# Gate weights of the first and third expert mixture fetched from device memory instead of formed by a matmul

## The reference, cut to what matters

```python
# layer 0 (32 experts of width 64, top 8, one shared expert), gate weights topk_w [rows, 8]
g = einsum('th,eih->eti', x, expert_gate); u = einsum('th,eih->eti', x, expert_up)
outs = einsum('eti,ehi->eth', silu(g) * u, expert_down)
final = (gathered * topk_w[:, :, None]).sum(1) + shared(x)
# layer 2 (32 experts, top 4, capacity 128 rows an expert), gate weights w
h = silu(xe @ W1) * (xe @ W3); ye = h @ W2
out = (ye[eid, posc] * gflat[:, None]).reshape(-1, K, D).sum(1) + shared(X)
```

## Time and profile before

| | |
|---|---|
| median of 3 runs | 866.2 us (862.1 to 868.02) |
| profiled execution | 867.06 us, span 865.3 us |
| PE / PEld busy | 759.5 us (88%) / 539.0 us (62%) |
| DVE busy | 553.4 us (64%) |
| ACT / POOL busy | 375.8 us (43%) / 390.4 us (45%) |
| mean granted PE clock | 0.939 of full speed |
| first W matmul / last W matmul | 120.2 us / 719.6 us after the start |

### The profile page before, as it was taken

How to read it: one execution, slowest core, us unless ns; L and a number is a source line. 1 busy time by engine, 2 the same in 40 slices (tenths; PEclk the granted TensorE clock), 3 DMA queues, 4 the chain that set the end, 5 groups by cost and what they waited for, 6 DMA issues and landing times.

```text
span 865.3 us, 13644 instructions
## 1 busy us (share of the span) xinstructions
PE 759.5 (88%) x3936; PEld 539.0 (62%) x3936; DVE 553.4 (64%) x1813; ACT 375.8 (43%) x834; POOL 390.4 (45%) x381
## 2 busy tenths in 40 slices
PE   6989889999999878976979787999989989798995
PEld 3467767676767546654969786565645544555663
DVE  3377877777788378862633575978776655344554
ACT  0234344444445435625545334547455565313441
POOL 2000024544546434363674343655445665253772
PEclk8799989999999969966999998999999999899999
DMA  5021899930000121014677651000330000013325
GB/s 146 1 62 50 267 333 332 333 88 0 1 1 1 53 57 30 21 47 146 172 208 211 195 167 50 10 1 1 83 101 14 13 10 17 10 41 78 101 70 146
DMA packets 74394, 79.34 MB, mean 92 GB/s; under 512 B 17769, under 2 KB 61424, under 8 KB 74194
## 3 DMA queue, kind: packets, MB, share of 16 engines
q1 hardware_dynamic: 68112, 69.49, 27.8%
q0 software_dynamic: 5024, 8.54, 2.9%
q10 hardware_dynamic: 1186, 0.43, 0.2%
HBM read 40.48 MB, written 39.85 MB: 93 GB/s over the span
## 4 chain that ended last, share of the span: by engine, by line
PE 60%; DVE 22%; issue 7%; POOL 4%; ACT 3%; DMA 3%; SPq 1%; ACTq 0%; DVEq 0%; POOLq 0%
PE psum L1186 54%; PE psum L1635 1%; POOL s L754 1%; DVE hb L2328 1%; DVE hb L2329 1%; DVE hb L2326 1%; DVE mr L1984 1%; DVE const L1940 1%; POOL s L732 1%; PE psum L1245 1%; DMA chosen<-in_mask_1x1xSxS_ik 1%; DVE wk L1941 1%; PE psum L1373 1%; DVE l_lo L1900 1%; DMA l_hi<-y 1%
## 5 line engine op out<-in xcount | busy, mean ns | idle before, releaser
L1186 PE MATMUL psum<-xt_hi,wa_hi 128*128 128x512 f32 x272 | 129.0, 474 | 9.7 <-DVE hb L2329 5.0
L691 POOL TENSOR_TENSOR h_lo<-hb,h_hi 128x512 fp32r<-128x512 f32 x68 | 87.7, 1293 | 83.1 <-ACT h_hi L920 82.8
L759 POOL DMA_INDIRECT y<-xn x93 | 92.2, 992 | 64.7 <-DVE xn L2076 33.6
L902 ACT ACTIVATE hb<-psum 128x512 f32<-128x512 f32 x136 | 81.0, 596 | 86.3 <-PE psum L1186 85.7
L1186 PE MATMUL psum<-xt_lo,wa_hi 128*128 128x512 f32 x272 | 108.4, 399 | 0.0
L686 POOL TENSOR_TENSOR hb<-hb,wsb 128x512 f32<-128x512 f32 x64 | 82.3, 1286 | 56.6 <-DVE hb L2326 51.5
L662 POOL TENSOR_TENSOR rstd<-veps,neghalf 128x4 f32<-128x4 f32 x20 | 20.3, 1017 | 130.0 <-DVE veps L1878 129.6
L1186 PEld LDWEIGHTS psum<-xt_hi,wa_hi 128*128 128x128 f32 x272 | 52.7, 194 | 31.6 <-DVE hb L2329 9.5
L2326 DVE TENSOR_TENSOR hb<-hb,psum 128x512 f32<-128x512 f32 x68 | 46.0, 684 | 40.0 <-ACT hb L902 29.5
L1186 PE MATMUL psum<-hb,wa_hi 128*128 128x512 f32 x136 | 70.9, 602 | 0.5 <-POOLq L688 0.5
L1186 PEld LDWEIGHTS psum<-xt_lo,wa_hi 128*128 128x128 f32 x272 | 52.5, 193 | 16.2 <-issue 7.5
(11 more groups left out here) (353 smaller groups left out, 1706.9 us busy)
## 6 DMA issues: line engine op xcount, KB each, us to landing
s<-l_lo SPq DMA_DIRECT2D x20, 1386.0 KB, 16.5
l_hi<-in_pack SPq DMA_DIRECT2D x24, 322.0 KB, 3.4
l_lo<-in_pack SPq DMA_DIRECT2D x22, 322.0 KB, 3.4
xn<-s SPq DMA_DIRECT2D x93, 66.0 KB, 2.0
stage<-in_pack SPq DMA_DIRECT2D x13, 256.0 KB, 2.7
y_in<-y SPq DMA_DIRECT2D x8, 256.0 KB, 3.8
l_hi<-y SPq DMA_DIRECT2D x8, 256.0 KB, 4.9
stage<-in_L_ffn_W SPq DMA_DIRECT2D x12, 128.0 KB, 2.4
```

The source lines that it names most:

```text
L691: pool.tensor_tensor(h_lo[:, k % 3, :], hb[:, k % 4, :], h_hi[:, k % 3, :].bitcast(F32), ALU.subtract).then_inc(q["hlo_pool"], 1)
L759: pool.indirect_dma_start(y3, bass.IndirectOffsetOnAxis(xe3[:, j % XE, 128:129].bitcast(I32), 0), xe3[:, j % XE, 0:128], None, bounds_chec ...
L902: act.activation(hb[:, k % 4, :], G[k % 2][:, :], ACT.Silu).then_inc(q["sg_done"], 1)
L1186: return pe.matmul(o, l, r, start=start, stop=stop, skip_group_check=True)
```

## The change

- `comb_in` turns the f32 weights `wfin` (32 rows) in place of the three bf16 parts; `route_end` is one instruction in layer 0 and ends one product after the capacity test in layer 2.
- `pre_comb` copies them to `wt0`; a DMA writes `wt0` to a new tensor `wd` in device memory (SP issues it for layer 0, ACT for layer 2), and SP then reads, for each routed unit, two rows of `wd`, each repeated over 64 partitions, into SBUF: eight buffers `wrow` in layer 0, the three buffers `wsb` in layer 2.
- The W matmul, its PSUM banks, `comb_t` and ACT's copy of W go away. In layer 0 the freed banks make G and U three deep, and DVE multiplies by `wrow` (SBUF). In layer 2 POOL multiplies by `wsb` as before, but waits for the DMA.
- The shared expert becomes the first chunk of a sequence.
- The 20 pattern fills are spread: 3 first, then 4 in each of three sequences, then 5. The loads of layer 3's weights go from SP to ACT, at unit 40 of layer 2.
- Routing steps of layer 2 and the Fourier steps that lie in it are put in other units; in the `chain` everything from `pt` on comes one step later.

```diff
-            back1=42, rows5=42, upd1=43, xt5=44, low5=45, logits5=46, score5=47, choose5=48, cum5=49, end5=50)
+            back1=42, rows5=42, upd1=43, xt5=44, low5=44, logits5=45, score5=46, choose5=47, cum5=48, end5=48, comb5=49)
-CH = dict(mom6=0, scl6=3, xt6=4, scores=5, exp=6, norm=7, pt=7, ptc=8, val=8, up=9, scl7=12, xt7=13, logits=14, top=15,
+CH = dict(mom6=0, scl6=3, xt6=4, scores=5, exp=6, norm=7, pt=8, ptc=9, val=9, up=10, scl7=13, xt7=14, logits=15, top=16,
...
+        G0, U0 = [bank[i] for i in (0, 1, 4)], [bank[i] for i in (2, 3, 5)]
...
+            return (c - 1, 15 + c, 31 + c) if c else (48, 49, 50)
...
-        ROUTE_AT = {0: (5, 6, 7, 9, 10, 11, 11, 12, 12), 2: (8, 8, 8, 8, 8, 9, 10, 11, 12)}
-        WEIGH_AT = {0: 13, 2: 14}
-        COMBT_AT = {0: 15, 2: 16}
-        PE_XN, PE_LOGITS, PE_RUN, PE_COMB = {0: 0, 2: 2}, {0: 1, 2: 5}, 11, {0: 12, 2: 13}
+        ROUTE_AT = {0: (5, 6, 7, 9, 10, 11, 11, 12, 12), 2: (8, 8, 8, 8, 8, 9, 9, 9, 10)}
+        WEIGH_AT = {0: 13, 2: 11}
+        COMBT_AT = {0: 15, 2: 13}
+        PE_XN, PE_LOGITS, PE_RUN, PE_COMB = {0: 0, 2: 2}, {0: 1, 2: 5}, 8, {0: 13, 2: 10}
...
-                return 2 + b, (4, 7, 8, 11, 10, 13)
+                return 2 + b, (6, 9, 12, 14, 14, 16)
...
+            def gate_rows(b, c):
+                w = b * ROUTED[0] + c
+                if w >= WS:
+                    pb, pc = divmod(w - WS, ROUTED[0])
+                    sp.wait_ge(q["h_done"], hnum(0, pb, pc + 1) + 1)
+                for e in range(2):
+                    sp.dma_start(wrow[64 * e:64 * e + 64, w % WS, :],
+                                 wd[b, 2 * c + e:2 * c + e + 1, :].broadcast_to([64, S])).then_inc(d_wb[w % WS], 16)
+
+            def gate_weights():
+                ...
+                for b in range(B):
+                    sp.wait_ge(q["combt_done"], fnum(0, b))
+                    sp.dma_start(wd[b], wt0[:, :]).then_inc(d_wt, 16)
+                    sp.wait_ge(d_wt, WT0 + 16 * (b + 1))
+                    for c in range(ROUTED[0]):
+                        gate_rows(b, c)
+                        if b + 1 < B and c in Z_AFTER:
+                            zero_rows(Z_FIRST + b * len(Z_AFTER) + Z_AFTER.index(c))
...
+            for b in range(B):
+                sp.wait_ge(d_wt2, WT2 + 16 * (b + 1))
+                for c in range(ROUTED[2]):
+                    w = b * ROUTED[2] + c
+                    if w >= 3:
+                        sp.wait_ge(q["w_used"], w - 2)
+                    for e in range(2):
+                        sp.dma_start(wsb[64 * e:64 * e + 64, w % 3, :],
+                                     wd[b, 2 * c + e:2 * c + e + 1, :].broadcast_to([64, S])).then_inc(d_w1[w % 3], 16)
...
-                    pool.wait_ge(q["wcopy_done"], w + 1)
+                    pool.wait_ge(d_w1[w % 3], WB2[w % 3] + 32 * (w // 3 + 1))
...
+                act.activation(wt0[:, :], T[0:32, :], ACT.Copy).then_inc(q["combt_done"], 1)
+                if l == 2:
+                    act.wait_ge(q["combt_done"], fnum(l, b))
+                    act.dma_start(wd[b], wt2[:, :]).then_inc(d_wt2, 16)
...
+            def load_layer3():
+                act.wait_ge(q["x_done"], x_num(4, 3))
+                for i, w in enumerate(("routed_w1", "routed_w2", "routed_w3")):
+                    act.dma_start(pk3[:, :, F3 * i:F3 * i + F3], a["L3_ffn_" + w].rearrange("e d h -> d e h")).then_inc(d_wl, 16)
...
+                if l == 0:
+                    if k >= 3:
+                        pe.wait_ge(q["sg_done"], k - 2)
+                    product(G0[k % 3][:, :], gs).then_inc(q["g_done"], 1)
+                    if k >= 3:
+                        pe.wait_ge(q["um_done"], k - 2)
+                    product(U0[k % 3][:, :], us).then_inc(q["u_done"], 1)
+                    return
...
-                    last = mm(W[0 if l == 2 else k % 2][:, :], pick, comb_t[0:3 * N_EXP[l], b % 2, :], True, True)
...
+                if l == 0:
+                    dve.tensor_tensor(wfin[:, :, :], w_, wrec[:, :].unsqueeze(2).broadcast_to([128, TB, E]),
+                                      ALU.mult).then_inc(q["comb_done"], 1)
+                    return
...
-                for j in range(2):
-                    link(dve.tensor_copy(chl[:, :, E * j:E * j + E], w_))
-                    ...
+                    dve.tensor_tensor(wfin[:, :, :], w_, m_, ALU.mult).then_inc(q["comb_done"], 1)
...
-                    link(dve.tensor_tensor(h, h, U[k % 2][:, :], ALU.mult))
-                    dve.tensor_tensor(h, h, W[k % 2][:, :], ALU.mult).then_inc(q["h_done"], 1)
+                dve.tensor_tensor(h, h, U0[k % 3][:, :], ALU.mult).then_inc(q["um_done"], 1)
+                ...
+                dve.wait_ge(d_wb[w % WS], 32 * (w // WS + 1))
+                dve.tensor_tensor(h, h, wrow[:, w % WS, :], ALU.mult).then_inc(q["h_done"], 1)
```

More of the change, by code:

```diff
@@ L53 @@
 ROWS_AHEAD = 3
+Z_FIRST = 3
+Z_AFTER = (8, 10, 12, 14)
 ZR = 3
@@ L95 @@
 SH_DOWN = {SH_AT + t: n for n, t in enumerate((11, 17, 22))}
-COUNT_PE = [SH_AT + t for t in (17, 18, 19)]
+COUNT_PE = [SH_AT + t for t in (18, 19, 20)]
 C_ID, C_HEAD, C_TRI, C_SEL, C_SEL16, C_SEL8, C_DFT = 0, 128, 144, 272, 304, 320, 328
@@ L210, in link, with build @@
         self.eng.wait_ge(self.sem, self.n)
-def build(nc, a, out, s1, s3, y3, stages=8):
+def build(nc, a, out, s1, s3, y3, wd, stages=8):
     with ExitStack() as ctx:
@@ L308, in build @@
         d_x = [sem(f"d_x{b}") for b in range(B)]
+        d_wt, WT0 = d_wnat, 16 * 4
+        d_wb, W1_BASE = d_w1, 32 * (B * ROUTED[0] // WS)
+        d_wt2, WT2 = d_wnat, 16 * (4 + B)
+        WB2 = [W1_BASE + 16 * len(range(i, NB1, WS)) for i in range(3)]
         d_stage = [sem(f"d_stage{i}") for i in range(2)]
@@ new lines, in gate_rows @@
+            def gate_rows(b, c):
[7 more added lines that the diff above has]
+            def gate_weights():
+                sp.wait_ge(q["zp_set"], 2)
+                for i in range(Z_FIRST):
+                    zero_rows(i)
+                for b in range(B):
[6 more added lines that the diff above has]
+                            zero_rows(Z_FIRST + b * len(Z_AFTER) + Z_AFTER.index(c))
@@ L565, in _ @@
             for r in range(NQ):
                 if r == NQ0:
-                    sp.wait_ge(q["zp_set"], 2)
-                    for rows, s in ((ROWS1 // 128, s1), (ROWS3 // 128, s3)):
-                        flat = s.rearrange("(p r) c -> p (r c)", p=128)
-                        for z in range(0, rows, ZCHUNK):
-                            n = min(ZCHUNK, rows - z)
-                            dst = flat[:, ROW3 * z:ROW3 * (z + n)].rearrange("p (r c) -> p r c", c=ZR * ROW3)
-                            sp.dma_start(dst, zpat.unsqueeze(1).broadcast_to([128, n // ZR, ZR * ROW3])).then_inc(d_zero, 16)
+                    gate_weights()
@@ L574, in _ @@
                 if r == NQ0 + 2:
+                    for i in range(Z_FIRST + (B - 1) * len(Z_AFTER), NZ):
+                        zero_rows(i)
                     sp.wait_ge(q["x_done"], x_num(1, 3))
@@ L1107, in _ @@
                         context_out(i)
+                        if stages > 1 and i == 15:
+                            pre_comb(0, 0)
                         if i < 12:
@@ L1153, in _ @@
                             k = b * NC[l] + c
[L1154 to L1156 removed]
+                            if l == 2 and k == L3_AT:
+                                load_layer3()
+                            if l != 2 and k >= 1:
                                 pb, pc = divmod(k - 1, NC[l])
@@ L1418, in comb_in @@
             def comb_in(l, b):
-                rows = 3 * N_EXP[l]
                 pe.wait_ge(q["comb_done"], fnum(l, b))
@@ L1422, in comb_in @@
                 for k in range(TB):
-                    last = pe.transpose(T[:, :].bitcast(BF16)[0:rows, 128 * k:128 * k + 128], chl[:, k, 0:rows], ident_bf[:, :])
+                    last = pe.transpose(T[0:32, 128 * k:128 * k + 128], wfin[:, k, :], ident)
                 last.then_inc(q["combt_ps"], 1)
@@ L1762, in _ @@
                             values0(i - 1)
+                        if stages > 1 and i == 15:
+                            comb_in(0, 0)
                         if i < 12:
@@ L2640 @@
     y3 = nc.dram_tensor("y3", (2 * B * S, D), F32, kind="Internal").ap()
-    build(nc, a, out, s1, s3, y3, STAGES)
+    wd = nc.dram_tensor("wd", (B, 32, S), F32, kind="Internal").ap()
+    build(nc, a, out, s1, s3, y3, wd, STAGES)
     r = run_bass_kernel_spmd(nc, [arrays], core_ids=[0])
```

112 lines of the change are left out of this document (41 added, 71 removed).

## The result

The changed kernel is slower: 884.34 us median (879.78 to 894.81, four runs) against 864.15 for the kernel before on the same chip; the ratio is 1.020, 95% interval 1.0158 to 1.0242. The forecast was 852 us.

A forecast was written before the change was run, and what follows sets the result against it. PE was taken to bound most of both mixtures, DVE next. Terms -8, -1.2, -8.7, -1.5, -2, +1.5 and +6 sum to -13.9; 867.1 less 13.9 and 0.9 (profiled execution above median) gives 852 us, range 828 to 870.

The forecast's parts named there:

- Layer 0, -8: Layer 0: W matmuls and split go, DVE's gate product and POOL take turns; sequences of 43.2 us, -8 us in all.
- The bound for PE alone: Layer 0: a sequence takes 39.0 us if PE alone decides, without the W matmuls.
- The fetch in layer 0, 0: Layer 0: gate rows' round trip of 6.2 us is covered by 1 us; 0, range 0 to +9 us.
- Entry of layer 2, -1.2 and "0, at worst +3": Layer 2's start: split leaves PE's path, -1.2 us; first gate row's round trip hides behind other units, 0, at worst +3.
- POOL's wait for gate rows, +1.5: Layer 2: POOL waits for a DMA with three buffers, 1.52 us a unit; +1.5 us, range 0 to +9.
- W matmuls, -8.7: Layer 2: 64 W matmuls leave PE, three quarters of 11.7 us taken; -8.7 us, bounds -14.4 and -4.
- ACT's loads, +6 (0 to +13): Layer 2, unit 40: ACT issues layer 3's loads, silu stands behind them; +6 us, range 0 to +13.
- Moved steps, 0: Layer 2: routing and Fourier steps in other units, two units of lead; 0, range -2 to +4 us.
- the chain shift: Chain steps one later, in stage 7; 0, range -2 to +2 us.
- the split and ACT's copy (-3.5): Layer 2: shorter split in three sequences, half on the path, -1.5 us; ACT's copy of W gone, -2 us.
- The slow rival: Layer 0: POOL starts before DVE asks in each routed unit, +18 and +1, less 6 in layer 2; 879 us, 12%.
- its ring: Layer 0, slow rival: gate product, ACT and POOL in a ring of 2.65 us a unit in place of 2.29.

The follow-up runs named there:

- layer 0's half alone: Layer 0 as in the changed kernel, layer 2 and its chain back as before the change; 867.5 us, ratio 1.0027.
- gates first: Changed kernel with gate rows of layer 2's first three routed units issued by SP ahead of the y_in loads; 882.9 us, ratio 1.0176.
- five edits: Changed kernel plus layer 0's silu in PSUM, its gate rows one unit earlier, layer 3's loads spread, layer 2's gate rows before y_in, y_in used later; 852.4 us.

## Why the prediction was wrong

**Layer 0, -8: failed.** The mechanism was right, the size was not. The gate product's mean came out as foretold (1.06 us over all, waits inside it), POOL's at 1.42; but a unit with routing beside it takes 3.0 us (nine units in 27 us from 224.9 us), not 2.7. My step let POOL's instruction fall either on the product or on a routing step; in two of these nine units both are hit (4.6 and 4.4 us), and three steps of 0.2 to 0.3 us become 1.2 to 1.4. So a sequence is 45 us and not 43.2. That is a third of the miss: from update to update of x (which lie at different units of their sequences) the middle two are 3 us over my sum (44.9 and 30.2 us with layer 0's half alone; before 44.8 and 30.6), the first is 4 over it (66.0; before 64.2) and the last 3 (34.9 in both). For the last I had taken 3 us because it has no routing, but DVE is busy there for 38.0 us in place of 33.5. The bound for PE alone was sound: without the subtraction sequences are 38 to 39.8 us. A slip beside this: my 23.4 us of products count 34 in a sequence that has 33, so 0.7 us of routing was missing. The Trainium skill, SBUF — State Buffer, section "SBUF: two separate sides", limits the lock to DVE instructions in a mode that uses both ports or with two inputs in SBUF; the silu left in PSUM agrees (0.69 us for 128 products). I had this rule and did not ask which operand could be kept out of SBUF.

**The fetch in layer 0, 0: right here** (DVE waits 0.9 us in sum), because DVE itself was late; once it is not, a border shows up to 2.7 us.

**Entry of layer 2, -1.2 and "0, at worst +3": wrong.** I had counted the round trip, but not SP's own queue: its first gate row stands behind a wait and four loads. The first gate row alone was not the cost, though (gates first: no change); with it first and `y_in` used two units later the layer is 3.2 us shorter (242.0 to 238.8, one trace against another). No run tests the -1.2. POOL's wait for gate rows, +1.5 in my sum, is 5.7 us in the changed kernel, 5.0 of them here at the entry.

**W matmuls, -8.7: failed.** Put back for PE they cost 4 to 6, near the bound of 4, and up to the last gate product the layer with five edits is 5.5 us shorter than before. I took PE's 58% of the chain for what would go; but the next path was close behind, and POOL's product lies on it (18 to 19 us without it): POOL was busy for 109.7 of 192 us, and its product, scatter and hand-overs take turns in one queue. I looked at DVE as the next bound and never summed POOL's queue by unit.

**ACT's loads, +6 (0 to +13): right mechanism, size 11.** The six issues took 13.3 us on ACT, a little more than SP's 10.6. What I left out is the clock: PE's 8.3 us of standing still are followed by 11.7 us at 1.2 GHz. The Trainium skill, DMA: Bandwidth & Descriptors, section "Issuing engines are not separate DMA queues", calls the issue time usually small relative to the DMA itself. The fourth load disagrees (5.98 us of issue, 10.8 from issue to landing), the spread loads agree (0.36 to 0.85 us, and 2.8 to 8.9 to landing).

**Moved steps, 0: the chain shift is mis-sized.** It puts 17 matmuls of PE behind the last gate product (253 for 236) and costs the tail 4.3 us at one granted clock; ahead of the tail the layer is some 7 us shorter with it in the first three sequences.

**Sum.** Foretold -13.9, measured +17 by the ratio. Of the 31 us between them layer 0 has about 10 (+2 for -8), the loads 5, W about 4, the entry 4, the chain in the tail 4; these are estimates from the runs above, each uncertain by 1 to 3 us. What is left, some 4, is of the size of the split and ACT's copy (-3.5), but no run separates it. The slow rival's 879 us was near the time and wrong in its place: its ring would have made sequences of 50.7 us and left layer 2 the gain. Layer 0 came out about even; layer 2 lost.

## What to carry to other kernels

Before work is taken from the engine that heads the chain, sum every other engine's queue per unit, with its scatters and hand-overs: the gain ends at the next one. Read the stretch and its tail apart: here one gained 5.5 us and the other gave 6.1 back. When an operand moves from PSUM to SBUF, look for an instruction of POOL beside it, and for another operand that could stay in PSUM instead. Transfers put on a computing engine's queue go one at a time, units apart.
